# A decoder of two layers on one core: fewer hand-written table loads on ScalarE, and one norm applied by VectorE from the bank

## Time and profile before

| | before |
|---|---|
| median of 3 runs | 3151.66 us (3150.8 to 3157.52) |
| profiled execution | 3149.89 us, its span 3147.8 us |
| granted TensorE clock, mean | 0.85 of full |
| busy: PE, DVE, ACT, POOL | 2395.0, 2461.9, 1234.9, 1054.0 us |
| table loads on ScalarE, in `rstd`, at `dt_exp`, in `dt_b` | 44, 12, 12, of 1283 ns each |
| DMA | 339.60 MB, mean 108 GB/s |

### The profile page before, as it was taken

The page is one execution under the profiler, slowest core; times in us unless marked ns, Lnnn a source line. Parts: engine busy times, 40 slices in busy tenths (PEclk is TensorE's granted clock), DMA queues, the critical chain, the costliest instruction groups (busy, mean ns, idle before and its releaser), DMA issues.

```text
span 3147.8 us, 20459 instructions
## 1 busy us (share of the span) xinstructions
PE 2395.0 (76%) x6316; PEld 1147.8 (36%) x6316; DVE 2461.9 (78%) x1928; ACT 1234.9 (39%) x1970; POOL 1054.0 (33%) x291
## 2 busy tenths in 40 slices
PE   5687899228969876689688875896887838969965
PEld 1243333103424443334344433343443324445532
DVE  5997997998979998899799889897998993121132
ACT  4434454424353452552434534524345332021222
POOL 0342233354434445424344454244444530000000
PEclk7887999558979998699889987898899869979986
DMA  2125552202212764022116740221265502216920
GB/s 78 34 100 167 177 180 69 102 0 85 64 37 86 221 225 138 25 95 66 41 64 222 236 148 25 87 67 40 76 199 186 173 0 81 77 44 225 297 65 14
DMA packets 156573, 339.60 MB, mean 108 GB/s; under 512 B 30448, under 2 KB 47856, under 8 KB 151792
## 3 DMA queue, kind: packets, MB, share of 16 engines
q1 hardware_dynamic: 130864, 261.41, 26.4%
q10 hardware_dynamic: 20480, 60.10, 5.2%
q0 software_dynamic: 5120, 16.78, 1.6%
HBM read 296.16 MB, written 57.54 MB: 112 GB/s over the span
## 4 chain that ended last, share of the span: by engine, by line
PE 38%; DVE 32%; issue 14%; ACT 8%; POOL 3%; DMA 3%; ACTq 0%; SPq 0%; DVEq 0%; POOLq 0%
DVE hb L1523 12%; PE ps L719 6%; PE ps L902 6%; PE ps L764 5%; PE ps L909 5%; DVE hb L1531 4%; DVE hb L1436 4%; POOL ya L1802 2%; DMA ring<-in_w_edn 2%; PE ps L1036 2%; PE ps L945 2%; PE ps L832 2%; PE ps L875 1%; DVE sm L1379 1%; ACT T L1318 1%
## 5 line engine op out<-in xcount | busy, mean ns | idle before, releaser
L1802 POOL TENSOR_TENSOR ya<-ya,hb 128x2048 f32<-128x2048 f32 x188 | 857.6, 4562 | 1383.0 <-DVE hb L1523 1326.5
L1523 DVE TENSOR_TENSOR_SCAN hb<-da,hb 128x2048 f32<-128x2048 f32 x192 | 858.5, 4471 | 2.3 <-ACT da L1076 0.7
L1076 ACT ACTIVATE da<-dl,pk 128x511 f32<-128x511 f32 x768 | 489.3, 710 | 453.8 <-DVE hb L1523 445.7
L1436 DVE TENSOR_TENSOR hb<-du,ps 128x2048 f32<-128x2048 f32 x192 | 436.1, 2271 | 35.0 <-POOL ya L1802 26.1
L1531 DVE TENSOR_TENSOR hb<-hb,ps 128x2048 f32<-128x2048 f32 x192 | 437.6, 2279 | 3.6 <-PE ps L849 2.9
L764 PE MATMUL ps<-V,ring 128*128 128x512 f32 x512 | 237.7, 620 | 30.7 <-DVE V L1464 18.1
L729 PE MATMUL ps<-bct,sel 64*128 64x512 f32 x192 | 106.3, 554 | 191.5 <-DVE hb L1436 181.9
L719 PE MATMUL ps<-ring,hid 128*128 128x512 f32 x544 | 246.8, 610 | 3.8 <-DVE hid L1568 3.1
L926 PE MATMUL ps<-ring,hid 128*128 128x352 f32 x480 | 194.9, 489 | 14.4 <-ACT hid L1289 7.9
L930 PE MATMUL ps<-ring,hid 128*128 128x352 f32 x480 | 190.2, 479 | 13.0 <-ACT X L1306 12.9
L902 PE MATMUL ps<-T,ring 128*128 128x512 f32 x352 | 167.6, 621 | 28.7 <-DVE T L1556 19.4
(11 more groups left out here) (265 smaller groups left out, 3324.8 us busy)
## 6 DMA issues: line engine op xcount, KB each, us to landing
ring<-egu SPq DMA_DIRECT2D x240, 352.0 KB, 3.9
ring<-in_w_edn SPq DMA_DIRECT2D x72, 512.0 KB, 5.5
ring<-in_w_fgu SPq DMA_DIRECT2D x44, 512.0 KB, 3.7
ring<-in_w_in SPq DMA_DIRECT2D x32, 512.0 KB, 4.0
hid<-xrows SPq DMA_DIRECT2D x60, 256.0 KB, 4.4
yrows<-X ACTq DMA_DIRECT2D x60, 256.0 KB, 4.6
ring<-in_w_egu SPq DMA_DIRECT2D x24, 512.0 KB, 3.3
ring<-in_w_edn SPq DMA_DIRECT2D x60, 192.0 KB, 4.4
```

The lines of the kernel that those rows point to most:

```text
L1076: i = act.activation(dav(n % 2)[:, k, 1:], dl[:, k, 1:], ACT.Exp, scale=Aneg[:, (4 * (u % 3 - 1) if u % 3 else UC) + k, m:m + 1])
L1436: dve.tensor_tensor(hbv(m % NHB), du[:, :, :], wide(ps[:, 5, :], 4), ALU.mult).then_inc(s["dbu"], 1)
L1523: dve.tensor_tensor_scan(hb[:, h, :], da[:, b % 2, :], hb[:, h, :], 0.0, ALU.mult, ALU.add)\
L1802: pool.tensor_tensor(sums, ya[:, :, :], hbv(m % NHB), ALU.add).then_inc(s["acc"], 1)
```

## The change

A variable on the building side, `cnt["table"]`, remembers whether the last table put in by hand is still the one loaded: tasks that use Tanh set it to "tanh" as they are reached in ScalarE's order, and `tables()` loads only where it isn't "log". All three places call `tables()`.

For n = 0 ScalarE stops after `rstd`; a new VectorE task, `ln_y`, waits for r4 and writes `nat = (ps + (-mean)) * r4` with four TENSOR_SCALARs, each of which releases a tangent of the gate. The four shifts and the four passes of ScalarE go. In `plan()` norm 0 costs ScalarE 2.2 instead of 5.6 us, `ln_y` 2.8 us on VectorE, and the gate may start 2 us before its end.

```
-       "mm": KC, "x1": KC, "resid": 1, "xn": KC, "sq": 5, "stat": 1, "rstd": 8, "xe": 16, "bst": 15, "shift": 5, "nrm": 4 * TT,
+       "mm": KC, "x1": KC, "resid": 1, "xn": KC, "sq": 5, "stat": 1, "rstd": 8, "xe": 16, "bst": 15, "shift": 4, "nrm": 4 * TT,
...
-            chain(30, ("ln", b, n), [("dve", us + 0.3), ("act", 5.6)], at)
+            chain(30, ("ln", b, n), [("dve", us + 0.3), ("act", 5.6 if n else 2.2)], at)
+            if n == 0:
+                put(30, ("ln_y", b, 0), "dve", 2.8, (("ln", b, 0), "act"))
+                return ("ln_y", b, 0), "dve"
...
-        chain(30, ("gate", b, 0), [("act", 2.4), ("dve", 5.6), ("pe", 3.6)], (("ln", b, 0), "act"), (("sb", NST * (3 * b + 1) - 1, 0), "pool"))
+        chain(30, ("gate", b, 0), [("act", 2.4), ("dve", 5.6), ("pe", 3.6)], (("ln_y", b, 0), "dve", -2), (("sb", NST * (3 * b + 1) - 1, 0), "pool"))
...
-                cnt = {"ln": 0, "h_ln": 0}
+                cnt = {"ln": 0, "h_ln": 0, "table": ""}
+
+                def tables():
+
+                    if cnt["table"] != "log":
+                        act.preload_act_table_set("natural_log_exp_and_others")
+                        cnt["table"] = "log"
...
-                    act.preload_act_table_set("natural_log_exp_and_others")
+                    tables()
                     act.activation(dst, src, ACT.Ln, bias=c("eps", eps, 1, parts), scale=scale).then_inc(s[pre + "ln"], 1)
...
                 for t, b, n in order["act"]:
+                    if t in ("p_th", "c_th", "p_gz", "ffn_ev", "exp_ev", "bh", "gate"):
+                        cnt["table"] = "tanh"
...
                     elif t == "dt_exp":
-                        act.preload_act_table_set("natural_log_exp_and_others")
+                        tables()
...
                             act.wait_ge(s["scan"], NST * b - 1)
-                        act.preload_act_table_set("natural_log_exp_and_others")
+                        tables()
...
                         rstd(r4, mv[:, :, 1], "t", 1)
+                        if n == 0:
+                            continue
...
-                        act.wait_ge(*of("shift", b, n + 1))
-                        for e in range(TT):
-                            act.activation(nat[:, e, :], (nat if n else ps)[:, e, :], ACT.Identity, bias=shift[:, e:e + 1],
-                                           scale=r4[:, e:e + 1]).then_inc(s["nrm" if n else "v"], 1)
+                        act.wait_ge(*of("shift", b, n))
+                        for e in range(TT):
+                            act.activation(nat[:, e, :], nat[:, e, :], ACT.Identity, bias=shift[:, e:e + 1],
+                                           scale=r4[:, e:e + 1]).then_inc(s["nrm"], 1)
...
+                    elif t == "ln_y":
+                        dve.wait_ge(*of("rstd", b, 2))
+                        for e in range(TT):
+                            dve.tensor_scalar(nat[:, e, :], ps[:, e, :], mv[:, e, 0:1], r4[:, e:e + 1], ALU.add, ALU.mult)\
+                                .then_inc(s["v"], 1)
```

## The result

The changed kernel takes 3159.86 us (median of 22 runs, 3152.63 to 3163.85), the kernel before in the same rounds 3153.59 (22 runs, 3145.66 to 3161.18). The ratio is 1.0018, 95% interval [1.0012, 1.0025]: about 6 us slower. The forecast was 3129, range 3114 to 3143.

What follows compares the result with a forecast made beforehand. Scans fill VectorE until about 2600 us, then sequence 3 runs alone as a dependent chain. Seven gains sum to 25.4 us, less 2.8 slip, 22.6 off the profiled 3149.89: 3127.3, as a median 3129 us, range 3114 to 3143.

Steps and rivals of the forecast that it cites:

- What it adds and moves: New `ln_y` work and order: scan goes ahead of the gate, VectorE loses nothing, a later chain costs 2.8 us.
- Rival 2: New order eats half the gain: full 5.6 us slip plus one 9.1 us VectorE idle, 3141 us; chance 0.14.
- Rival 3: Slower: the gate's eight VectorE instructions get blocked behind GpSimd's adds, 26 us for three gates, 3158 us; chance 0.06.
- The signs: Wrong if loads return, VectorE idle before 2600 us doesn't fall, or last `fin` to sequence 3's first FFN grows over 5.6 us.
- a): `dt_b` at a unit's start: without its load, VectorE's next instruction ends 0.74 us earlier in nine units, 6.7 us.
- b): `dt_exp` of units 6 and 9: a load left out ends VectorE idling for `dt_b` earlier, 2 x 1.28 = 2.6 us.
- c): Gates of sequences 0 to 2: VectorE runs `ln_y` instead of idling, 0.46 us each, 1.4 us in all.
- d): `bias_d` of sequences 0 and 1: VectorE's 1.88 us idle behind a load shrinks, 2 x 1.28 = 2.6 us.
- e): `ln` 3 of three sequences: its load, which leads on to later work, goes, 3 x 1.28 = 3.9 us.
- f): Tail: loads of `seg_r`, `ln` 3, `ln` 4 and `bias_d` leave the chain, 4 x 1.28 = 5.1 us.
- g): Gate of sequence 3: time from r4 to the first gate instruction falls from 5.74 to 2.7 us, gain 3.1.
- The drain rule: Rival: each load on the path takes 1.38 us more away, 12.4 us on terms d to f, 3117 us; chance 0.02.

Runs made afterwards that it cites:

- e8: Changed kernel in its own order, with four silus (`c_th`) moved in VectorE's list for sequences 2 and 3: 3145.27 us, ratio 0.9972 to the kernel before.
- e1: Changed kernel with the orders planned as before, `ln_y` directly ahead of the gate: 3135.25 us, ratio 0.9941 to the kernel before.
- e9: Kernel before's order with the new table rule, norm 0 applied by VectorE for sequence 3 alone: 3136.43 us, ratio 0.9942 to the kernel before.
- e3: Kernel before with `ln_y` alone, old order, all 68 hand loads kept: 3150.47 us, ratio 0.9989 to the kernel before.
- e2: Kernel before with the table rule alone, no `ln_y`, old order: 3135.2 us, ratio 0.9939 to the kernel before.
- e12: Changed kernel in its own order, with four silus moved and `att_end` put behind the products: 3133.48 us, ratio 0.9936 to the kernel before.

## Why the prediction was wrong, step by step

**The step that failed** is the claim under "What it adds and moves" that with the scan ahead of the gate "VectorE loses nothing". I walked the new order only as far as the gate. Behind it the tasks of the unit's first eight scans stand elsewhere among the scans, and that put silus of `c_th` into GpSimd's adds: 14.5 us (e8) of the 24 us that the whole order costs (changed kernel against e1), where I had 2.8. The 2.8, a slip of sequence 2's chain into the tail, were not there at all: the statistics of its `ln` 3 start 16.77 us ahead of the last `fin` before and 16.76 in the changed kernel. (That the gate's new place is what moved the silus is argued from the lists; no run moves the gate alone.) Rival 2 named the planner's interleaving, at 9.1 us, and came out at 3141. Rival 3 had the mechanism and its price for one instruction right, but looked for it at the gate's eight instructions and set its deciding point there. Those were not blocked at all:

```profile
908.58 2.85 DVE L1517 SCALAR_TENSOR_TENSOR hb<-hb,da 128x2048 f32<-128x2048 f32 x1 [8.64 <-ACT da L1259]
...
915.99 2.96 DVE L1626 TENSOR_SCALAR T<-ps,mv,sm 128x512 f32<-128x512 f32 x4
...
921.25 4.42 DVE L1536 TENSOR_TENSOR_SCAN hb<-da,hb 128x2048 f32<-128x2048 f32 x1
925.59 0.67 DVE L1632 SCALAR_TENSOR_TENSOR T<-T 128x512 f32<-128x512 f32 x1
```

This is unit 4 of the changed kernel. The order is the one that I had walked, and the gates end 26.3 us after the Exp's end (26 forecast). The chance of 0.06 was far too low: the rows of blocking show some 4.3 us for a single instruction, and an order moves many of them.

**The signs** that I had named missed it. Loads did not come back, VectorE's idle time before 2600 us fell (busy 2362.4 us there instead of 2331.3), and from the last `fin` to the statistics of norm 0 of sequence 3 it is 179.98 us instead of 180.34. Yet the last `fin` starts 15.5 us later (2614.10 against 2598.63), where 12 to 17 us earlier was forecast: the loss lies in the length of instructions, and I had watched only idle time.

**The terms**, in the changed kernel or, where its order hides them, in e9 or e1:
- a) Exact where the pattern holds: L1517 waits 8.64 us and takes 2.85 here, and ends 6.75 us after the Exp's end instead of 7.49 in units 0 to 4, 6, 7, 9 and 10. In units 8 and 11 of the changed kernel `fin` and the add of `dl` and `hb` start together, as they did in unit 5 before:

```profile
1772.78 4.52 POOL L1805 TENSOR_TENSOR dl<-dl,hb 128x2048 f32<-128x2048 f32 x1
1772.85 6.60 DVE L1550 SCALAR_TENSOR_TENSOR yg<-ya,yg 128x2048 f32<-128x2048 f32 x1 [6.96 <-POOL ya L1820]
```

  and in unit 5 they no longer do: a coincidence that moves from unit to unit with the order.
- b) Not separated by any run. In units 6 and 9 the idle time ahead of `dt_c` fell from 7.04 and 6.34 us to 4.60 and 4.20; less `dt_b`'s 1.28 that leaves 1.2 and 0.9 us, forecast 1.28 each.
- c) 0.26 us each in e1 (2.80 from the end of `dt_c` to the gate, against 3.06), forecast 0.46, since an `ln_y` takes 0.72 us in a row and not 0.62. The loads alone would have given 1.95 each, so the norm on VectorE costs 1.7 us per gate.
- d) Exact: 1.88 us of idling fell to 0.60, both times.

```profile
1396.63 2.74 DVE L1569 SCALAR_TENSOR_TENSOR T<-V,pk,R 128x512 f32<-128x512 f32 x4 [0.60 <-ACT sm L1079]
```

- e) For sequence 2 1.08 us of 1.28 (statistics of `ln` 3 to those of `ln` 4: 28.82 to 27.74).
- f) 3.4 of 5.1 us: `seg_r` 2.2 (more than its load), `ln` 3 0.3, `ln` 4 and `bias_d` together 0.9 of 2.56. TensorE gave some back. The last 34 us before the output, kernel before and changed kernel (the granted clock is the number behind the bracketed counts, as a share of full), with one group of products:

```profile
3101.54:3136.29 34.75, 17.32 (x60) 11.50 (x60) 10.94 (x37) 12.39 (x23) 0.00 (x0) 0.57 0.00 1
...
L1043 PE MATMUL ps<-pk,X 128*128 128x64 f32 x32 | 5.4, 348 | 2.2 <-ACT X L1323 2.2
```

```profile
3113.90:3147.78 33.88, 19.02 (x60) 13.21 (x60) 10.95 (x37) 9.83 (x21) 0.00 (x0) 0.52 0.00 1
...
L1046 PE MATMUL ps<-pk,X 128*128 128x64 f32 x32 | 7.1, 423 | 2.2 <-ACT X L1336 2.2
```

  ScalarE is 2.56 us less busy, TensorE 1.7 us more with the same 60 products, at a granted clock of 0.52 instead of 0.57, both near the lower of its two levels (0.5, 1.2 GHz): 1.7 of the 2.56 us go there, and these 32 small products alone take 1.7 us longer. It is not the chance of one execution: e3 and e1 differ in nothing but the loads, and from the statistics of `ln` 4 to those of `bias_d` e3 takes 33.0 us at a granted clock of 0.62 with TensorE busy for 17.3, e1 33.4 us at 0.57 with 19.0. How the loads that are left out lower the clock isn't shown.
- g) 2.8 us, forecast 3.1: from r4 to the gate 2.92 instead of 5.74, of which `ln_y` is nearly all.

```profile
2798.84 0.20 ACT L1079 ACTIVATE sm<-sm 128x4 f32<-128x4 f32 x1
2799.08 2.97 DVE L1626 TENSOR_SCALAR T<-ps,mv,sm 128x512 f32<-128x512 f32 x4 [1.89 <-ACT sm L1079]
2801.96 0.68 DVE L1632 SCALAR_TENSOR_TENSOR T<-T 128x512 f32<-128x512 f32 x1
```

**The other rivals.** Loads did not come back (56 in all). The drain rule would have made e2 larger than the sum of the rows; it came out smaller. The 1.31 us of the earlier trace rows stand around a load of a set that was loaded already; a real switch looks the same: in e9 ScalarE's norm of sequence 0 ends at 913.05 and the tangent behind its load starts at 914.36.

## What to carry to other kernels

When an edit changes the costs from which an order is planned, the order is part of the change: walk the engine's list until it rejoins the old one, and for each instruction ask which instruction of the engine that shares its ports runs beside it. Time the edit once with the old order and once with the new; here the edit was worth 19 us and its order cost 24 us. On an engine that is full, an instruction's duration against its usual one is a better place to look than its idle time.

## What the runs showed of the hardware that I had not expected

Which of two instructions is held isn't always told by the recorded starts. In the changed kernel:

```profile
2277.71 9.00 DVE L1536 TENSOR_TENSOR_SCAN hb<-da,hb 128x2048 f32<-128x2048 f32 x1
...
2277.89 4.53 POOL L1820 TENSOR_TENSOR ya<-ya,hb 128x2048 f32<-128x2048 f32 x1
```

The scan has the earlier start by 0.18 us and yet ends 4.29 us behind the add, as if it had run wholly after it (its usual time is 4.42). In e8 and e12 it took 8.98 us at the same scan. And one tensor input in SBUF is enough to be held: the scaling of the softmax row, in e9:

```profile
2307.46 4.85 DVE L1697 TENSOR_SCALAR R<-R,sm 128x512 f32<-128x512 f32 x1
2307.50 4.52 POOL L1818 TENSOR_TENSOR ya<-ya,hb 128x2048 f32<-128x2048 f32 x1 [4.76 <-DVE hb L1534]
```
